# Conditions loaded straight to 128 partitions, and half of the products by 128x128 block diagonals

## The reference, cut to what matters

```python
w = weights[itok_B_1_198]                        # (64, 64, 64)
y = x + jnp.einsum('bct,bcd->bdt', x, w)         # x: (64, 64, 512)
```

## Time and profile before

| what | us |
|---|---|
| median of three executions | 48.42 |
| the profiled execution's own time | 48.91 |
| its span, first to last instruction | 47.0 |
| TensorE busy | 16.9 |
| VectorE busy | 13.7 |
| ScalarE busy | 9.4 |
| GpSimd busy | 1.7 |

### The profile page before, as it was taken

The page is one execution under the profiler, slowest core; times in us unless marked ns, Lnnn a source line. Parts: engine busy times, 40 slices in busy tenths (PEclk is TensorE's granted clock), DMA queues, the critical chain, the costliest instruction groups (busy, mean ns, idle before and its releaser), DMA issues.

```text
span 47.0 us, 351 instructions
## 1 busy us (share of the span) xinstructions
PE 16.9 (36%) x128; PEld 7.0 (15%) x128; DVE 13.7 (29%) x20; ACT 9.4 (20%) x9; POOL 1.7 (4%) x9
## 2 busy tenths in 40 slices
PE   0000000000000005999999999999980000000000
PEld 0000000000000002232333554544610000000000
DVE  1006100000000893003609559559658000000000
ACT  0730000000000000003408448547647000000000
POOL 4000530000000000000000000000000000000000
PEclk9999999999999999999999999999999955555555
DMA  0679999999999999999999999999999999999800
GB/s 0 111 328 432 425 425 404 439 432 432 446 411 404 439 432 432 418 397 425 439 425 425 404 425 425 439 418 397 425 425 418 404 418 439 418 411 411 341 28 7
DMA packets 2451, 17.84 MB, mean 379 GB/s; under 512 B 274, under 2 KB 274, under 8 KB 274
## 3 DMA queue, kind: packets, MB, share of 16 engines
q1 hardware_dynamic: 2304, 16.78, 86.4%
q0 software_dynamic: 144, 1.05, 5.3%
q10 hardware_dynamic: 2, 0.00, 0.0%
HBM read 9.44 MB, written 8.39 MB: 379 GB/s over the span
## 4 chain that ended last, share of the span: by engine, by line
PE 36%; DMA 22%; issue 9%; DVE 8%; POOL 1%; POOLq 1%
PE product L110 36%; DMA gathered<-weights,table_row 22%; DVE w_all L137 5%; DVE y_sb L142 3%; POOL piece L92 1%; DVE gathered L134 1%; POOLq L29 1%; POOLq L151 0%
## 5 line engine op out<-in xcount | busy, mean ns | idle before, releaser
L110 PE MATMUL product<-x_sb,w_all 64*64 64x512 f32 x128 | 16.9, 691 | 18.1 <-DVE w_all L137 18.1
L86 ACT COPY y_sb<-product 128x1024 f32<-128x1024 f32 x8 | 8.1, 1014 | 25.2 <-PE product L110 25.2
L142 DVE COPY y_sb<-product 128x1024 f32<-128x1024 f32 x8 | 9.8, 1225 | 8.4 <-PE product L110 8.4
L110 PEld LDWEIGHTS product<-x_sb,w_all 64*64 64x64 f32 x128 | 7.0, 204 | 27.3 <-DVE w_all L137 18.1
L134 DVE TENSOR_TENSOR gathered<-gathered,piece 128x64 f32<-128x64 f32 x1 | 0.3, 270 | 10.5 <-DMA gathered<-weights,table_row 10.5
L137 DVE STREAM_TRANSPOSE w_all<-gathered 128x2048 f32<-128x2048 f32 x1 | 2.3, 2311 | 0.0
L86 ACT ACT_TABLE_LOAD x1 | 1.3, 1283 | 1.5 <-DVE condition L117 1.5
L124 DVE STREAM_TRANSPOSE condition_of<-condition 32x32 int32<-32x32 int32 x4 | 0.8, 202 | 2.5 <-DMA condition<-conditions 2.4
L94 POOL DMA_INDIRECT gathered<-weights,table_row x1 | 1.1, 1072 | 3.9 <-DVE table_row L128 3.9
L92 POOL MEMSET piece<- 32x1 f32 x4 | 0.4, 92 | 0.5 <-POOLq L151 0.3
L117 DVE MEMSET condition<- 32x64 int32 x1 | 0.1, 112 | 0.8 <-PEq L151 0.8
## 6 DMA issues: line engine op xcount, KB each, us to landing
x_sb<-x SPq DMA_DIRECT2D x8, 1024.0 KB, 14.2
out<-y_sb SPq DMA_DIRECT2D x8, 1024.0 KB, 7.1
condition<-conditions ACTq DMA_DIRECT2D x1, 0.2 KB
gathered<-weights,table_row POOLq DMA_INDIRECT x1, 10.2
```

Source lines behind the costliest of these rows:

```text
L86: nc.scalar.copy(y_sb[:, 4 * turn:4 * turn + 2, :], product[turn % SETS][0][:, :, :]).then_inc(moved_by_act, 1)
L110: product_of = nc.tensor.matmul(product[turn % SETS][h][halves(g), j, :], w_all[halves(h), :, n], x_sb[halves(h), n, :], start=True, stop= ...
L142: nc.vector.tensor_copy(y_sb[:, 4 * turn + 2:4 * turn + 4, :], product[turn % SETS][1][:, :, :]).then_inc(moved_by_dve, 1)
```

## The change

The host pads the conditions: a (2, 32, 16) array of int32 in which each condition is alone on a line of 64 bytes. The kernel loads lines straight to the partitions, with two DMAs on ACT's queue, one for each half of the partitions. A half's source reads its 32 lines twice (a step of zero and a count of two outermost), so 64 partitions get 64 bytes each. The clearing, the four transposes and two semaphores go.

The second half of the turns (4 to 7) uses one call per pair, with a 128x128 weight matrix that holds the two samples' matrices on its diagonal and zeros elsewhere. The zeros are set by GpSimd and VectorE at the start, and ScalarE copies the matrices of turn 4 + t to their places in turn t, for t from 0 to 3. This makes 32 + 16 = 48 matmul calls. The output of the second half has another layout in memory, which the host undoes.

```diff
-        condition = sbuf("condition", [Q, B], i32)
-        condition_of = sbuf("condition_of", [P, Q], i32)
+        condition_of = sbuf("condition_of", [P, LINE], i32)
+        w_diag = sbuf("w_diag", [P, PAIRS - 4 * TILED, PAIR * D], fp32)
...
         @block.scalar
-            act.wait_ge(condition_cleared, 1)
-            act.dma_start(condition[0:1, :], conditions).then_inc(condition_loaded, 16)
+            for h in range(PAIR):
+                act.dma_start(condition_of[halves(h), :],
+                              bass.AP(conditions.tensor, h * Q * LINE, [[0, K], [LINE, Q], [1, LINE]])
+                              ).then_inc(condition_loaded, 16)
             for turn in range(TURNS):
+                if turn < TILED:
+                    later = slice(4 * turn, 4 * turn + 4)
+                    act.wait_ge(w_ready, 1)
+                    for h in range(PAIR):
+                        nc.scalar.copy(w_diag[halves(h), later, h * D:(h + 1) * D],
+                                       w_all[halves(h), :, pairs_of(TILED + turn)].rearrange("p d n -> p n d")
+                                       ).then_inc(w_placed, 1)
                 act.wait_ge(multiplied, turn + 1)
...
         @block.gpsimd
+            pool.wait_ge(pieces_set, 2 * (P // Q))
+            nc.gpsimd.memset(w_diag[halves(1), :, 0:D], 0.0).then_inc(w_zeroed, 1)
             pool.wait_ge(rows_known, 1)
...
         @block.tensor
+                if turn == TILED:
+                    pe.wait_ge(w_zeroed, 2)
+                if turn >= TILED:
+                    pe.wait_ge(w_placed, PAIR * (turn - TILED + 1))
                 for j in range(2):
                     for g in range(2):
+                        n = 4 * turn + 2 * j + g
+                        if turn >= TILED:
+                            product_of = nc.tensor.matmul(product[turn % SETS][j][:, g, :], w_diag[:, n - 4 * TILED, :],
+                                                          x_sb[:, n, :], start=True, stop=True)
+                            continue
                         for h in range(PAIR):
...
         @block.vector
-            nc.vector.memset(condition[:, :], 0).then_inc(condition_cleared, 1)
...
-            dve.wait_ge(condition_loaded, 16)
-            for q in range(P // Q):
+            nc.vector.memset(w_diag[halves(0), :, D:PAIR * D], 0.0).then_inc(w_zeroed, 1)
 
-                nc.vector.transpose(condition_of[q * Q:(q + 1) * Q, :], condition[:, q // K:B:PAIR]
-                                    ).then_inc(condition_turned, 1)
+            dve.wait_ge(condition_loaded, 16 * PAIR)
             dve.wait_ge(pieces_set, 2 * (P // Q))
-            dve.wait_ge(condition_turned, P // Q)
...
+    conditions = np.zeros((PAIR, B // PAIR, LINE), np.int32)
+    conditions[:, :, 0] = np.asarray(itok_B_1_198).reshape(B // PAIR, PAIR).T
```

More of the change, by code:

```diff
@@ L50, in conditioned_residual_kernel @@
         condition_loaded = semaphore("condition_loaded")
-        condition_cleared = semaphore("condition_cleared")
         pieces_set = semaphore("pieces_set")
-        condition_turned = semaphore("condition_turned")
         rows_known = semaphore("rows_known")
@@ L105, in _ @@
                     pe.wait_ge(moved_by_dve, turn - SETS + 1)
+                if turn == TILED:
+                    pe.wait_ge(w_zeroed, 2)
+                if turn >= TILED:
+                    pe.wait_ge(w_placed, PAIR * (turn - TILED + 1))
                 for j in range(2):
                     for g in range(2):
+                        n = 4 * turn + 2 * j + g
[3 more added lines that the diff above has]
+                            continue
                         for h in range(PAIR):
-                            n = 4 * turn + 2 * j + g
                             product_of = nc.tensor.matmul(product[turn % SETS][h][halves(g), j, :],
```

16 lines of the change are left out of this document (11 added, 5 removed).

## The result

The changed kernel took 59.86 us (median; 59.54 to 62.69) against 48.60 us for the one before in the same comparison: 1.225 times as long, interval 1.214 to 1.237. The profiled execution took 59.94 us, with a span of 57.8 against 47.0. One of the four executions, that of 62.69 us, was a slow one (granted clock 0.91 against 0.99), and every ratio here, with its 95% interval, leaves out executions over 1.5% above the fastest of their kernel, while medians are of all. The two edits cost very different amounts: the loading of the conditions alone costs 10.4 us, the block diagonals alone about 1 us.

The account below looks back on a forecast made before the run. Transfers bound the kernel before, TensorE 6.0 us ahead. Turn 3's products at 28.20, four turns of 3.44, move and issue 1.29, landing 4.3, end 0.35, conditions 1.3, beside the span 1.9, less 0.5 and 0.43: 50.1 us; own range 48.9 to 51.3, full 47.5 to 65.0.

Parts of the forecast that it names:

- The conditions: Loading at the start: 128 small packets alternate with the input's, so row numbers and first product come 1.3 us later.
- two engines: Rival at the conditions' load: 66 small packets on each engine, row numbers 14.6 us late, 63.9 us in all; chance 0.26.
- The forecast's own case: Conditions' load: packets spread over 16 engines, 10 each, first at 2.8 us, row numbers at 6.0 instead of 4.72; chance 0.34.
- The slower second half: Products of turns 4 to 7: 8 steps, 3.44 us a turn, 13.8 us for four, 6.9 more than before.
- the weight load: 128-column load in turns 4 to 7: at most 0.42 us, within a step, taken as nothing; upper end 1.6 us.
- both clearings: VectorE's and GpSimd's zeroing at the start: hidden, costing nothing unless GpSimd's takes beyond 3.7 us.
- ScalarE's copies: Two in each of turns 0 to 3, 0.25 to 1.0 us each, overrunning idle time by up to 1.3 us: nothing.
- The 6 us of slack: TensorE against the transfers at the end: it is 6.0 us ahead and may lose that much for nothing.
- third rival: Second-half products: whole-array calls as cheap as quarters, four turns in 6.9 us, transfers set the end, 48.4 or 47.1; chance 0.09.
- The last output: End of the kernel: the queue has run dry, so it lands alone, 4.3 to 4.8 us after issue; 4.3 taken.
- Laggard: Tail of the transfers: a single DMA engine still at work after the others, costing up to about 1.3 us.
- the fetch: Instruction fetch by one DMA engine at 35.1 us, 0.93 us; 192 instead of 256 matmul and weight-load instructions may spare it.

Follow-up runs that it names:

- the conditions alone: The changed kernel's loading of the conditions with all 64 matmul calls in quarters as in the kernel before; 58.81 us, 1.215 times before.
- diagonals alone: The kernel before with only the block diagonals of turns 4 to 7 added, conditions loaded as before; 49.69 us against 48.44.
- the gap in the source: Single load of 128 lines on 16 engines, its source given a gap after 64 lines so its outermost count is 2; 59.48 us, one execution.
- copies moved: Kernel before plus block diagonals of turns 4 to 7, with ScalarE's copies moved to where ScalarE is idle; 48.67 us against 48.84 for before.
- input later: The changed kernel with SyncE starting the input only when the conditions have landed; 51.21 us, one execution.

## Why the prediction was wrong

**The conditions** are the step that failed. The prediction took "if 128 packets spread over 16 engines" for its own case and put two engines among the rivals at 0.26. The packets ran on two. The row numbers came at 17.0 us instead of 6.0: the first packet started at 4.66 instead of 2.8, some 27 of an engine's 66 passed by 5.1, and the other 39 or 40, 0.31 us each, lasted until 16.5. The number of engines is the larger error, not the only one. The forecast's own case, two DMAs on 16 engines, was run too: row numbers at 7.66 instead of 6.0 and 52.18 us instead of 50.1, above the forecast's own range of 48.9 to 51.3, mainly since the packets started at 4.55. The single DMA of 128 lines came close to both numbers (5.86 and 49.82 us), but in part by luck: it started at 2.34 us and had nine packets an engine instead of ten. The 0.32 us that a small packet waits was costed right; the number of engines and the start were not. The rule for it was at hand, and the prediction quotes it: the Trainium skill, "DMA: Bandwidth & Descriptors", section "Rules for kernel authors", says that a leading zero-stride broadcast of c copies confines a DMA to at most c engines. The runs agree, with 132 packets for c = 2, and the gap in the source shows that the count does it, not the zero step. It deserved the larger chance, since nothing in the rows spoke against it.

**The rival's own size** was off too: row numbers at 24.1 by its sum, 17.0 measured. It had each of 66 packets wait for one of the input's; some 27 an engine passed freely. Its gather, put at 5.4 us, took 8.4, since the input filled the engines until about 24.5 us. These two errors of 7.1 and 3.0 us lie on opposite sides, which is why its 63.9 us were only 4 too many. The rule of the Trainium skill, same page, section "Queues, rings and completion order", of a whole packet of about 9 to 17 descriptors drained at a time, which the prediction set aside, may be behind such a burst, though this one has 27 to 31; that it is, no run here shows. From 5.1 us on the rows show one for one, so the rule does not describe this queue throughout. Why two engines' packets start at 4.65 us and 16 engines' in one DMA at 2.3 is open: two DMAs on 16 engines started late as well (4.55).

**The slower second half** was right: 3.44 us a turn, 3.43 measured; no cost for the weight load (0.19 us for 128 columns, no longer than for 64); both clearings hidden at 0.95 and 0.91 us.

**ScalarE's copies** were costed at nothing. They take 0.64 us each, two in every turn, so in turns 1 to 3 its moves came later and later (its copy of turn 3 at 39.48, VectorE's at 37.95), and TensorE's turn 4 lost 0.4 us on a path that had no slack left. The overrun had been worked out, up to 1.3 us; what was missed is that it adds up over turns.

**The 6 us of slack** were worked out at the end of the kernel, and the prediction's third rival lets the conditions use them. They hold for slower products late on: two turns of block diagonals, 3.4 us more, left the span at 45.5 and 45.7 us. They do not hold for a late start: the conditions alone came 12.3 us late, the first product 10.2, and the execution took 10.4 us longer. The forecast itself charged the conditions in full, so its sum does not rest on this.

**The last output** went as forecast, alone, but landed 3.8 us after issue instead of 4.3.

The forecast's span of 49.2 us, corrected term by term: conditions 17.0 - 6.0 = +11.0; gather 8.4 instead of 10.2, -1.8; turns 0 to 3 in 37.95 - 28.63 = 9.3 instead of 28.20 - 18.12 = 10.1, -0.8, as the steps became 0.43 us apart 4.8 us after the first product instead of 6.0; turns 4 to 7 in 52.25 - 37.95 = 14.3 instead of 13.8, +0.5; landing -0.5. That makes 57.6; the span was 57.8. The -1.8 and the -0.8 made the miss smaller without having been foreseen, and the second is chance: the spacing changed 3.4, 4.8 and twice 6.0 us after the first product in four traces (diagonals alone, changed kernel, before, copies moved).

**Laggard.** That fewer instructions may spare the fetch fits the traces, but its worth in time was not shown.

## What to carry to other kernels

Before a small load goes out beside a large one, work out how many packets it makes and over how many engines its outermost count spreads them; each of an engine's small packets may wait 0.3 us for a large one, so one packet and four VectorE transposes (row numbers at 4.72 us) can beat 128 direct ones (5.86 at best). A source whose outermost count was 2 put its packets on two engines, with a zero step and with a real one; counts of 64 and 128 used all 16. And where slack is to be spent, as TensorE's 6 us here, ask where on the path it lies: 3.4 us more in the last turns cost nothing that could be measured, while a first product that came 10.2 us late cost 10.4, since the transfers had run out of work.

## What was not expected of the hardware

With nothing beside them (input later), the 33 small packets that a DMA put on each of two engines took 0.3 us (66 in all from 2.1 to 2.45 us, and the second DMA's 66 from 3.15 to 3.5); with the input the two DMAs' packets lasted until 16.5 us. A load of 4-byte conditions came 1.0 us later than one of 64-byte lines on as many packets, in one trace of each. A 128x128 fp32 weight load took 0.19 us and a 64x64 one 0.20.
